# Attention sums to their channels by DMA, in place of transposes to tokens and back

## What is computed

```python
q, k, v = heads(xn @ Wq + bq), heads(xn @ Wk + bk), heads(xn @ Wv + bv)
y = softmax(causal(q @ k.T * scale)) @ v
y = y + softmax(qc @ kc.T * scale) @ vc          # kc, vc from ctx_512
x = x + y.reshape(B, T, C) @ Wp + bp
shared = silu(xf @ w1.T) * (xf @ w2.T) @ w3s.T
gates = sigmoid(xf @ router_w.T) * top2_mask
routed = sum_e((silu(h1_e) * h2_e * gates_e) @ w3_e.T)
x = x + shared + routed
```

## Time and profile before

| | us |
|---|---|
| three runs, median | 494.05 |
| the same runs, lowest and highest | 489.95, 494.63 |
| the profiled execution, from its first instruction to its last | 492.7 |
| PE busy in it | 458.7 |
| DVE busy in it | 368.1 |
| ACT busy in it | 224.2 |
| POOL busy in it | 69.9 |

### The profile page before, as it was taken

How to read it: one execution, slowest core, us unless ns; L and a number is a source line. 1 busy time by engine, 2 the same in 40 slices (tenths; PEclk the granted TensorE clock), 3 DMA queues, 4 the chain that set the end, 5 groups by cost and what they waited for, 6 DMA issues and landing times.

```text
span 492.7 us, 10634 instructions
## 1 busy us (share of the span) xinstructions
PE 458.7 (93%) x4141; PEld 341.3 (69%) x4141; DVE 368.1 (75%) x886; ACT 224.2 (45%) x356; POOL 69.9 (14%) x112
## 2 busy tenths in 40 slices
PE   0899999899999999999999999999999999998986
PEld 0666666567767776776777776777677777765876
DVE  3275676553977888797878788797888796887787
ACT  2225555435355454445545545455444545453211
POOL 7011101310013101220021101310032001210100
PEclk9999899955999999999999999999999999999999
DMA  6400000000000000000000000001000000000000
GB/s 158 114 13 0 1 18 12 1 1 17 2 12 1 12 18 11 0 0 27 0 11 0 17 10 11 0 0 27 0 2 1 23 2 1 1 23 2 1 12 11
DMA packets 15165, 7.04 MB, mean 14 GB/s; under 512 B 3608, under 2 KB 15008, under 8 KB 15136
## 3 DMA queue, kind: packets, MB, share of 16 engines
q1 hardware_dynamic: 13984, 6.43, 4.7%
q10 hardware_dynamic: 1152, 0.20, 0.2%
HBM read 5.58 MB, written 1.05 MB: 13 GB/s over the span
## 4 chain that ended last, share of the span: by engine, by line
PE 69%; DVE 18%; ACT 5%; issue 5%; DMA 1%; SPq 1%; POOLq 0%; DVEq 0%; POOL 0%; ACTq 0%
PE Bk L406 12%; PE Y L572 11%; PE Cb L406 11%; PE A L406 6%; PE S L429 4%; PE S L447 4%; PE S L453 4%; PE S L442 3%; PE Cb L655 3%; DVE shifts L1027 3%; ACT probs L780 3%; DVE acc L972 2%; PE Y L522 2%; DVE nat L862 2%; PE S L443 2%
## 5 line engine op out<-in xcount | busy, mean ns | idle before, releaser
L780 ACT ACTIVATE probs<-S 128x1024 f32<-128x1024 f32 (+1 forms) x128 | 110.9, 916 | 46.9 <-PE S L431 46.7
L789 ACT ACTIVATE qk<-Cb,one_row 128x512 fp32r<-128x512 f32 x62 | 42.6, 688 | 111.8 <-PE Cb L406 111.8
L1027 DVE TENSOR_REDUCE shifts<-S 128x4 f32<-128x1024 f32 x64 | 75.3, 1220 | 7.0 <-PE S L447 6.9
L572 PE MATMUL Y<-probs,vs 128*32 128x256 f32 (+1 forms) x1024 | 64.9, 373 | 3.3 <-DVE qk L1008 2.0
L1063 POOL TENSOR_SCALAR_AFFINE_SELECT probs<-probs 128x1024 f32<-128x1024 f32 x32 | 35.2, 1099 | 154.3 <-ACT probs L780 154.3
L406 PE MATMUL Cb<-nat,sel 128*128 128x256 f32 x248 | 48.5, 321 | 3.8 <-DVE nat L862 2.1
L1023 DVE TENSOR_REDUCE shifts<-S 128x2 f32<-128x512 f32 x64 | 44.0, 687 | 9.8 <-PE S L453 9.7
L406 PEld LDWEIGHTS Bk<-w3T,hid 128*128 128x128 f32 x336 | 40.7, 191 | 12.6 <-issue 8.1
L406 PE MATMUL Bk<-w3T,hid 128*128 128x128 f32 x336 | 48.3, 287 | 0.6 <-DVE hid L941 0.6
L572 PEld LDWEIGHTS Y<-probs,vs 128*32 128x32 f32 x1024 | 27.6, 113 | 26.0 <-DVE qk L1008 4.7
L767 ACT COPY yT<-Y 128x256 f32<-128x256 f32 x64 | 23.8, 372 | 44.1 <-PE Y L572 41.8
(11 more groups left out here) (159 smaller groups left out, 850.7 us busy)
## 6 DMA issues: line engine op xcount, KB each, us to landing
xin<-in_x_dram SPq DMA_DIRECT2D x8, 128.0 KB, 2.1
w_raw<-in_L_ffn_w_dram SPq DMA_DIRECT2D x4, 256.0 KB
xres<-in_x_dram SPq DMA_DIRECT2D x8, 128.0 KB, 2.4
out_dram<-acc SPq DMA_DIRECT2D x8, 128.0 KB, 1.8
cin<-in_ctx_dram SPq DMA_DIRECT2D x8, 64.0 KB, 1.9
w_raw<-in_L_ffn_shared_w_dram SPq DMA_DIRECT2D x4, 128.0 KB
w_raw<-in_L_ffn_w_dram SPq DMA_DIRECT2D x1, 512.0 KB
w_raw<-in_L_ffn_shared_w_dram SPq DMA_DIRECT2D x1, 256.0 KB
```

The source lines that it names most:

```text
L572: mm = nc.tensor.matmul(Y[QUAD * j:QUAD * (j + 1), q0:T], vs[:, kind, kt, GH * g + j, :], probs[u % 2][:, j, kt * T:(kt + 1) * T - q0], st ...
L780: nc.scalar.activation(probs[s % 2][:, hs, 0:kept(s)], S[:, hs, 0:kept(s)], ACT.Exp, scale=SCALE).then_inc(exped[s], 1)
L789: nc.scalar.activation(qk[:, u, :, :], bank_of(turn, f"place{u}")[:, :].rearrange("p (i t) -> p i t", i=2), ACT.Identity, bias=one_row[:, ...
L1027: nc.vector.tensor_reduce(dst.rearrange("p q j -> p j q"), S[:, hs, :].rearrange("p j (q k) -> p j q k", q=NT), AX_X, ALU.max, negate=True ...
```

## The change

The head's 32 rows are filled in another pattern: its 8 weighted values stand in rows 0, 4, 8, ..., and the sum of weights stands eight times, in rows 1, 5, 9, ... Each fourth row of `yT` is then already one channel of one head, and the row behind it holds the sum that belongs to it. SP sends them, unit by unit, with two DMAs of 32 rows by 256 tokens to `y_parts`: channels on 128 partitions, one plane of values and one of sums, per kind. The division is now done there, for 128 channels by 256 tokens: `invert` is a DVE reciprocal of a whole plane, once per kind; for kind x POOL multiplies, for kind c DVE (`merge`), and DVE adds the kinds straight into `y_sumT`. The steps `tokens0` to `tokens3` and `yT` are gone from the PE, with their DVE passes.

```diff
-EARLY = [("xT", 1), ("tokens3", -1), ("yT", -1), ("vc", 0), None, ("v", 1), ("qkc", 1), None]
-LATE = [("tokens2", -1), ("qk", 1), ("out", -1), ("x2T", -1), ("cT", 1), ("route", -1), ("tokens0", 0), ("tokens1", 0)]
+EARLY = [("xT", 1), None, None, ("vc", 0), None, ("v", 1), ("qkc", 1), None]
+LATE = [None, ("qk", 1), ("out", -1), ("x2T", -1), ("cT", 1), ("route", -1), None, None]
-        recip = sb("recip", [P, H])
-        y_tok = sb("y_tok", [P, 2, NT, C])
-        y_sum = sb("y_sum", [P, NT, C])
+        y_parts = sb("y_parts", [P, 2, 2, T])
+        recip = sb("recip", [P, 2, T])
+        y_kind = sb("y_kind", [P, 2, T])
# SP
+            def gather(turn, u, o=0):
+                if not turn.has(o):
+                    return
+                kind, g = divmod(u, NG)
+                if o == 0:
+                    wait(sp, yT_ready[u], turn.n(0))
+                    wait(sp, divided[kind], turn.n(-1))
+                else:
+                    wait(sp, divided[kind], turn.n(o - 1))
+                    wait(sp, yT_ready[u], turn.n(o))
+                for i in range(2):
+                    sp.dma_start(y_parts[g * QUAD:(g + 1) * QUAD, kind, i, :],
+                                 yT[i::SPREAD, u, :]).then_inc(gathered[kind], 16)
# PE: yT and tokens gone
-                    for g in range(NG):
-                        mm = nc.tensor.transpose(bank[:, g * P:(g + 1) * P],
-                                                 yT[:, NG * kind + g, tt * P:(tt + 1) * P], ident[:, :])
-                    mm.then_inc(tokens, 1)
                 elif name == "out":
-                    wait(pe, yT_sb, turn.n(o))
+                    wait(pe, merged, turn.n(o))
# ACT, before the copy to yT
+                    wait(act, gathered[u // NG], turn.n(o - 1, 32 * NG, 32 * NG))
# DVE
-                    nc.vector.reciprocal(recip[:, :], heads[:, :, D]).then_inc(recip_ready, 1)
+            def invert(turn, kind, o):
+                wait(dve, gathered[kind], turn.n(o, 32 * NG, 32 * NG))
+                wait(dve, divided[kind], turn.n(o - 1))
+                nc.vector.reciprocal(recip[:, kind, :], y_parts[:, kind, 1, :]).then_inc(recip_ready[kind], 1)
+            def merge(turn, o):
+                invert(turn, 1, o)
+                wait(dve, recip_ready[1], turn.n(o))
+                nc.vector.tensor_tensor(y_kind[:, 1, :], y_parts[:, 1, 0, :], recip[:, 1, :],
+                                        ALU.mult).then_inc(divided[1], 1)
+                wait(dve, divided[0], turn.n(o))
+                wait(dve, divided[1], turn.n(o))
+                nc.vector.tensor_tensor(y_sumT[:, :], y_kind[:, 0, :], y_kind[:, 1, :], ALU.add).then_inc(merged, 1)
                     from_bank_c(turn, LATE[s])
+                    if s == 1 and turn.has(-1):
+                        merge(turn, -1)
+                    if s == 5 and turn.has(0):
+                        invert(turn, 0, 0)
# POOL
-                        wait(pool, normed, turn.n(-1, 4, 4))
-                        nc.gpsimd.tensor_tensor(y_sum[:, :, :], y_tok[:, 0], y_tok[:, 1], ALU.add).then_inc(y_summed, 1)
+                    if s == 6 and turn.has(0):
+                        wait(pool, recip_ready[0], turn.n(0))
+                        wait(pool, merged, turn.n(-1))
+                        nc.gpsimd.tensor_tensor(y_kind[:, 0, :], y_parts[:, 0, 0, :], recip[:, 0, :],
+                                                ALU.mult).then_inc(divided[0], 1)
```

More of the change, by code:

```diff
@@ L21 @@
 QUAD = P // GH
+SPREAD = QUAD // D
 EXPERTS, HID, SHARED = 8, 128, 512
@@ L79 @@
               + [(p, -1) for p in range(PAIRS)])
-DRAIN = ([("values", 0), ("hidden", 0), ("bank_c", "tokens2"), ("hidden", 1), ("bank_c", "tokens3"), ("w3", 0),
-          ("hidden", 2), ("bank_c", "yT"), ("w3", 1), ("hidden", 3), ("bank_c", "out"), ("w3", 2),
+DRAIN = ([("values", 0), ("hidden", 0), ("hidden", 1), ("w3", 0),
+          ("hidden", 2), ("merge", 0), ("w3", 1), ("hidden", 3), ("bank_c", "out"), ("w3", 2),
           ("warm", 16), ("bank_c", "x2T"), ("w3", 3), ("hidden", 4), ("bank_c", "route"), ("hidden", 5), ("w3", 4)]
@@ L283, in attention_moe_program @@
         SUM_STEPS = [1] * SHARED_PAIRS + [2 * NT] * (PAIRS - SHARED_PAIRS)
-        masked = [sem(f"masked{u}") for u in range(NG)]
+        masked = sem("masked")
         ln1 = sem("ln1")
@@ L310, in attention_moe_program @@
         c_free = {f"place{u}": (qk_ready[u], 1, 1) for u in range(UNITS)}
-        c_free |= {f"tokens{i}": (normed, i + 1, 4) for i in range(4)}
         c_free |= {"xT": (xT_lo, 1, 1), "vc": (v_ready[1], 1, 1), "v": (v_ready[0], 1, 1),
-                   "yT": (yT_sb, 1, 1), "qk": (proj_lo[0], 2, 2), "qkc": (proj_lo[1], 2, 2),
+                   "qk": (proj_lo[0], 2, 2), "qkc": (proj_lo[1], 2, 2),
                    "out": (ln2, 1, 7), "cT": (cT_lo, 1, 1), "x2T": (x2T_lo, 1, 1),
@@ L383, in one_turn @@
                     load_x(t + 2)
+                gather(turn, UNITS - 1, -1)
+                for u in (0, 1, 2):
+                    gather(turn, u)
                 if turn.has(-2):
@@ L387, in one_turn @@
                     sp.dma_start(out[t - 2].rearrange("(t p) c -> p t c", p=P), acc[:, :, :]).then_inc(out_sent, 16)
+                gather(turn, 3)
                 if turn.loop or 0 <= t + 2 < B:
@@ L395, in one_turn @@
                     sp.dma_start(xres[:, :, :], x[t].rearrange("(t p) c -> p t c", p=P)).then_inc(xres_in, 16)
+                for u in (4, 5, 6):
+                    gather(turn, u)
             turns(sp, one_turn)
@@ L564, in values @@
                     if u < NG:
-                        wait(pe, masked[u], turn.n(o))
+                        wait(pe, masked, turn.n(o, u + 1, NG))
                     kind, g = divmod(u, NG)
@@ L617, in bank_c @@
                     mm.then_inc(x2T_ps, 1)
-                elif name == "yT":
-                    wait(pe, y_summed, turn.n(o))
-                    wait_bank(pe, turn, C_USES, c_free, name)
-                    for tt in range(NT):
-                        mm = nc.tensor.transpose(bank[:, tt * P:(tt + 1) * P], y_sum[:, tt, :], ident[:, :])
-                    mm.then_inc(yT_ps, 1)
                 elif name in ("qk", "qkc"):
@@ L649, in bank_c @@
                     mm.then_inc(v_ps[kind], 1)
-                elif name.startswith("tokens"):
-                    kind, tt = divmod(int(name[-1]), NT)
-                    wait(pe, yT_ready[NG * kind + NG - 1], turn.n(o))
-                    wait_bank(pe, turn, C_USES, c_free, name)
-                    for g in range(NG):
-                        mm = nc.tensor.transpose(bank[:, g * P:(g + 1) * P],
-                                                 yT[:, NG * kind + g, tt * P:(tt + 1) * P], ident[:, :])
-                    mm.then_inc(tokens, 1)
                 elif name == "out":
-                    wait(pe, yT_sb, turn.n(o))
+                    wait(pe, merged, turn.n(o))
                     wait_bank(pe, turn, C_USES, c_free, name)
@@ L717, in drain @@
                         fill(Y, i)
-                    else:
+                    elif step == "bank_c":
                         bank_c(turn, (i, -1))
@@ L865, in from_bank_c @@
                             op0=ALU.add, op1=ALU.subtract).then_inc(proj_lo[kind], 1)
-                elif name == "yT":
-                    wait(dve, yT_ps, turn.n(o))
-                    nc.vector.tensor_copy(y_sumT[:, :], bank[:, 0:T]).then_inc(yT_sb, 1)
                 elif name in ("v", "vc"):
@@ L1043, in one_turn @@
                     from_bank_c(turn, LATE[s])
+                    if s == 1 and turn.has(-1):
+                        merge(turn, -1)
+                    if s == 5 and turn.has(0):
+                        invert(turn, 0, 0)
             def drain(turn):
                 for step, i in DRAIN:
-                    if step == "hidden":
+                    if step == "merge":
+                        merge(turn, -1)
+                    elif step == "hidden":
                         activate(turn, LAST_PAIRS[i], i)
@@ L1098, in _ @@
             pool.wait_ge(built, 8)
-            nc.gpsimd.memset(vs[:, :, :, :, D:D + 1], 1.0).then_inc(consts, 1)
+            nc.gpsimd.memset(vs[:, :, :, :, 1::SPREAD], 1.0).then_inc(consts, 1)
             select(earlier[:, :, :], ALU.is_gt, 0.0, 0, [[1, EXPERTS], [-1, EXPERTS]], 0).then_inc(consts, 1)
```

23 lines of the change are left out of this document (6 added, 17 removed).

## The result

The changed kernel took 522.84 us (median of four runs, 520.08 to 531.34) against 493.26 for the kernel before beside it: 1.062 times as long, with a 95% interval of 1.054 to 1.071. It is slower by 6%, and lies beyond the upper end of the range. Medians in this document are of all runs of a kernel, ratios only of those within 1.5% of its fastest, so the two need not agree to the last tenth. The execution that was profiled is the longest of the four (531.34, a span of 529.6), at a mean clock of 0.888 where the other three (520.08, 520.95 and 524.72) have 0.923 to 0.937, so its slow stretches are together longer than theirs; its lines are read for places and waits, and the sizes are taken from the timed runs.

A forecast was written before the change was run, and what follows sets the result against it. PE, busy 93%, was taken as the bound, following DVE in slots 6, 2 and 3. Terms of +0.91 us per turn, with the ends, summed to +5.6: 492.7 to 498.3 profiled, 499.6 us as median; range 481 to 511.

The forecast's parts named there:

- The reciprocal: DVE's reciprocal of one 128x256 plane, once per kind: 1.7 us, from a fixed part of 158 ns and 6.0 ns per element.
- The transfers: DMAs from `yT` to `y_parts`: landing 2.1 us after issue, tightest cover 3.7 us before `merge`, so costing nothing.
- The waits: PE waiting for DVE's shift each turn: about 2 us in slot 2, and 1.6 us longer than before in slot 6.
- The sum without the clock: Whole run: +5.4 us in the loop turns, -1.1 in turns 0 and 1, +1.3 in the drain, together +5.6.
- slot 5 to 7: Slot 6: `invert` of kind x delays DVE's q and k of kind c, less the removed `tokens0`: +1.10 us per turn.
- slot 7 to 0: End of slot 7: `tokens1` removed from PE, 0.5 of its 0.58 us counted: -0.50 us per turn.
- slot 0 to 1: Slots 0 and 1: `tokens2`, and `tokens3` with its wait, removed from PE: -0.88 us per turn.
- slot 1 to 5: Slots 1 to 2: `merge` brings DVE to the pair's pass 1.63 us later, partly absorbed by slot 3: +1.19 us per turn.
- The clock: Rival, chance 0.10: PE's waits in slots 2 and 6 bring one more slow stretch, up to half of 24.6 us, so 511.
- If the clock falls in a loop turn: Stated sign of being wrong, beside PE's idle time in the loop not growing.
- the forecast and its neighbours: Forecast 499.6 us (0.46); cheap reciprocal 481.0 (0.11); DVE catching up at both seams 492.9 (0.20); dearer reciprocal 505.5 (0.13).
- PE's savings: Removed PE steps per turn: `tokens0` 0.53 us in slot 6, `tokens1` 0.50 in slot 7, `tokens2` and `tokens3` 0.88 in slots 0 and 1.

The follow-up runs named there:

- the fillers: Changed kernel plus 16 PE matmuls of constants that nothing reads, ahead of unit 7's placement in slot 2 each loaded turn: 499.12 us, 1.022 times the kernel before.

## Why the prediction was wrong, point by point

**The reciprocal** was right: 1.746 us against 1.7. The Trainium skill (VectorE: DVE Perf Modes, section "First, the fixed hardware budget") has a repeat count of 8, from which I had estimated 2.3 us; the measurement decides against that estimate: between 16 and 256 elements it is (1746 - 254) / 240 = 6.2 ns each.

**The transfers** were right: 1.8 us from issue to landing, never waited for, and nothing on the kernel before.

**The waits** were right in place and nearly in size. About 2 us were forecast in slot 2 and 2.06 measured. In slot 6 1.6 more than before were forecast; PE stood 1.16 for nat of kind c ahead of the placement, and then for the shift the 0.26 of before. The turn without the long dip, as the fillers leave it, is 55.2 us against 54.8.

**The sum without the clock** was too small by about 4 us. Runs at the same clock can be compared: the kernel before at 0.984 took 490.4, the changed one with fillers 499.6 at 0.986, 9.2 more where I had 5.6. The terms of one loop turn can be compared with the starts of the values, one per slot. Two of them in the timeline of PE, slots 5 and 6, for the kernel before and for the changed one with fillers:

```profile
286.21 1.07 PE L572 MATMUL Y<-probs,vs 128*32 128x256 f32 x16
294.37 1.07 PE L572 MATMUL Y<-probs,vs 128*32 128x256 f32 x16
...
281.86 1.07 PE L594 MATMUL Y<-probs,vs 128*32 128x256 f32 x16
291.69 1.34 PE L594 MATMUL Y<-probs,vs 128*32 128x256 f32 x16 [0.24 <-DVE qk L1019]
```

All slots, for one loop turn from slot 5 on (before from 286.21, with fillers from 226.66, changed from 238.54):

| from the values of one slot to those of another, us | before | with fillers | term measured | forecast | changed, no fillers |
|---|---|---|---|---|---|
| slot 5 to 7 | 13.99 | 15.21 | +1.22 | +1.10 | 16.43 |
| slot 7 to 0 | 6.03 | 5.72 | -0.31 | -0.50 | 5.71 |
| slot 0 to 1 | 7.54 | 6.63 | -0.91 | -0.88 | 6.64 |
| slot 1 to 5 | 26.40 | 27.64 | +1.24 | +1.19 | 32.72 |
| the turn | 53.96 | 55.20 | +1.24 | +0.91 | 61.50 |

So each term of the turn was within 0.2 us; the largest miss is that of `tokens1`. Six turns of 0.33 are 2.0 of the 3.6 us; the rest lies outside the loop's turns and isn't split. Moving the reciprocal of kind x made the kernel 14.5 us faster, and there the clock is in it again: over four turns, slot 2 to slot 2, the profiled executions differ by 9.9 us (223.97 and 214.10), of which 6.8 are four times the 1.7 of slot 6 and 3.1 lie behind the two dips of slot 6 that the fillers had left.

**The clock** is the step that failed. The forecast put what follows a wait of PE at nothing: it counted the 2 us of waiting in slot 2 and the 1.6 in slot 6 and no more. The clock stood only as a rival with a chance of 0.10 and a price of one more slow stretch in the whole run, "up to half of 24.6". The runs show a slow stretch behind slot 2 in every loop turn, and behind slot 6 in most. Without fillers the turn above is 6.3 us longer than with them, nearly all of it in the slots behind the two waits. The fillers, which leave the values of slot 2 where they were, give back 22 us, four fifths of the 28 that the changed kernel loses (520.95 less 493.26), or two thirds by the ratios, each beside its own runs of the kernel before (0.040 of 0.062). "If the clock falls in a loop turn" stood among the signs of being wrong, and that sign came. I had both halves of it in hand: the forecast of a 2 us wait each turn, and the clock of the kernel before, whose two slow slices in turn 1 follow gaps of PE. One of them, in the timeline of PE, and the windows from there on:

```profile
96.60 0.41 PE L622 MATMUL Cb<-ident,y_sum 128*128 128x128 f32 x2 [0.84 <-DVE nat L862]
...
96.00:100.00 4.00, 3.40 (x30) 2.19 (x34) 3.40 (x6) 1.62 (x3) 1.10 (x1) 0.88 0.02 4
100.00:104.00 4.00, 4.00 (x29) 2.75 (x21) 1.46 (x6) 1.64 (x3) 0.59 (x2) 0.50 0.00 0
```

The mistake was to take the one stretch as one event instead of as what can happen behind such a gap, once for every turn. What the traces don't give is a fixed price: a wait of some 2 us was followed by nothing, by 3 us or by 14 to 17. The chances followed: the forecast and its neighbours were counted without a price for PE standing idle beyond the idle time.

**What PE's savings were worth.** I subtracted 0.5 to 0.9 us a turn for the transposes taken away. In slots 7, 0 and 1, where DVE doesn't hold PE up, the turn did shorten, by 1.2 us in all. With the reciprocals on the kernel before, the loss is 18.7 us; with the rest of the change, the transposes taken away and `merge` longer by a pass, it is some 28. Not counted was that PE then comes earlier to a wait which DVE ends, so the work removed just ahead of it turns into a longer gap.

**The best version** found is the changed kernel with fillers in slot 2 and the reciprocal of kind x behind slot 7: 484.63 us, 1.2% (0.4 to 1.8%) less than before. That is a small gain; with kind c ahead of nat as well (486.29) the ratio is the same.

## What to carry to other kernels

When a change takes work from the busiest engine ahead of a wait that another engine ends, count the gap it leaves and what the clock may do behind that gap, once for every turn of the loop; a trace of the kernel before that shows one slow stretch behind a gap is the warning. The price of one such gap went from nothing to 17 us at half clock here, so it has to be measured: fillers in the gap alone, with the next real work no earlier, measure it. A long pass on a helper engine costs by what is queued behind it: moving one pass of 1.75 us two slots on, to where the helper is ahead, made the kernel with fillers 14.5 us faster. Fillers paid only where they could start when the wait began: ahead of the wait they won some 20 us, behind the late engine's semaphore they lost 17, and where there was no gap they lost 9.

## What the hardware showed that was not expected

A gap of 2.06 us in an otherwise busy PE was followed by some 14 us at a granted clock of 0.50, with PE at work throughout, and in other turns of the same execution by 3 us. A gap of 1.2 us in slot 6 was followed by a dip of 3 us in some turns and by none in others. A DVE pass of 128 float32 elements that writes every fourth column took 391 ns, against 286 when it writes eight neighbours at a time.
